# A graph network with a mixture of experts on one core: router spread and biases in packs of four row groups, and z added to x by transfers

## The reference, cut to what matters

```python
x = x + gnn(layernorm(x), ...)                 # the kernel keeps the two terms apart: x and z
t = layernorm(x)
hs = gelu(t @ sw1.T + sb1);  shared = hs @ sw2 + sb2.sum(0)       # 2 shared experts, width 64
probs = softmax(t @ gate_w.T + gate_b)                            # 8 experts
cw = probs where among the two largest, else 0                    # weights of a node
hr = gelu(t @ rw1.T + rb1);  routed = sum_e cw[e] * (hr[e] @ rw2[e] + rb2[e])
out = x + shared + routed
```

## Time and profile before

| | |
|---|---|
| runs, median (lowest to highest) | 1684.27 us (1680.18 to 1685.67) |
| profiled execution, its own time | 1692.14 us |
| its span, from first to last instruction | 1690.4 us |
| TensorE busy in the span, granted clock | 94%, 0.987 |
| VectorE, ScalarE, POOL busy | 54%, 43%, 30% |
| expert stage | about 983 to 1690 |

### The profile page before, as it was taken

The page is one execution under the profiler, slowest core; times in us unless marked ns, Lnnn a source line. Parts: engine busy times, 40 slices in busy tenths (PEclk is TensorE's granted clock), DMA queues, the critical chain, the costliest instruction groups (busy, mean ns, idle before and its releaser), DMA issues. The chain is left out here.

```text
span 1690.4 us, 24020 instructions
## 1 busy us (share of the span) xinstructions
PE 1592.6 (94%) x7903; PEld 1256.2 (74%) x7903; DVE 917.8 (54%) x2179; ACT 724.9 (43%) x1169; POOL 505.5 (30%) x570
## 2 busy tenths in 40 slices
PE   3999999989898999999999868999999999999998
PEld 2677766777785677778887747878888888888887
DVE  4555686967732333347655436664556555655543
ACT  2344435656531222235655324444344534443442
POOL 3572232567732000003665322221112211221100
PEclk9999999999999999999999978999999999999999
DMA  8999999577759999996777750311132113211201
GB/s 259 266 280 280 299 294 271 163 176 125 127 64 290 291 277 282 281 285 192 131 131 143 148 135 34 125 75 75 75 133 93 75 75 125 99 75 75 87 26 44
DMA packets 74133, 273.85 MB, mean 162 GB/s; under 512 B 12726, under 2 KB 12740, under 8 KB 58930
## 3 DMA queue, kind: packets, MB, share of 16 engines
q1 hardware_dynamic: 52530, 223.36, 41.4%
q0 software_dynamic: 21504, 49.26, 16.0%
HBM read 179.82 MB, written 92.76 MB: 161 GB/s over the span
## 5 line engine op out<-in xcount | busy, mean ns | idle before, releaser
L888 POOL TENSOR_TENSOR zr<-zr,xr 128x2048 f32<-128x2048 f32 (+1 forms) x19 | 89.3, 4703 | 414.1 <-DMA xr<-in_x 396.5
L927 ACT ACTIVATE th<-bank 128x512 fp32r<-128x512 f32 x158 | 94.4, 597 | 185.5 <-PE bank L1161 185.3
L1141 PE MATMUL bank<-tth,w1h 128*128 128x512 f32 (+1 forms) x400 | 165.6, 414 | 8.1 <-ACT gel L1064 8.1
L1141 PE MATMUL bank<-ttl,w1h 128*128 128x512 f32 (+1 forms) x400 | 157.8, 395 | 0.0
L1141 PE MATMUL bank<-tth,w1l 128*128 128x512 f32 (+1 forms) x400 | 156.9, 392 | 0.0
L1141 PE MATMUL bank<-w2h,gth 128*128 128x512 f32 x395 | 155.2, 393 | 0.5 <-DVE gtl L1656 0.5
L1141 PE MATMUL bank<-w2h,gtl 128*128 128x512 f32 x395 | 154.7, 392 | 0.0
L1141 PE MATMUL bank<-w2l,gth 128*128 128x512 f32 x395 | 154.3, 391 | 0.0
L1141 PE MATMUL bank<-root2h,th 128*128 128x512 f32 x316 | 132.2, 418 | 8.2 <-DVE yout L1456 4.6
L1141 PE MATMUL bank<-root1h,th 128*128 128x512 f32 x316 | 131.8, 417 | 7.0 <-DVE yout L1456 4.6
L1427 DVE SCALAR_TENSOR_TENSOR tl<-bank,th 128x512 fp32r<-128x512 f32 x79 | 54.5, 690 | 154.1 <-ACT th L927 154.0
(11 more groups left out here) (213 smaller groups left out, 3797.1 us busy)
## 6 DMA issues: line engine op xcount, KB each, us to landing
basis_t<-in_gnn_basis SPq DMA_DIRECT2D x64, 896.0 KB
xin<-in_x SPq DMA_DIRECT2D x39, 512.0 KB, 7.6
xin<-y SPq DMA_DIRECT2D x39, 512.0 KB, 7.1
xr<-in_x SPq DMA_DIRECT2D x19, 1024.0 KB, 6.9
zr<-z SPq DMA_DIRECT2D x19, 1024.0 KB, 4.9
out<-zr SPq DMA_DIRECT2D x19, 1024.0 KB, 3.9
y<-yout SPq DMA_DIRECT2D x37, 512.0 KB, 7.5
z<-yout SPq DMA_DIRECT2D x34, 512.0 KB, 6.8
```

Of the source, the lines that this page charges most:

```text
L888: pool.tensor_tensor(zq, zq, xr[:, q.mod(2), 0:n, :], ALU.add).then_inc(s_zx, 1)
L927: act.activation(th_a[:, s, :], tpb[s][:], f).then_inc(s_hi, 1)
L1141: ins = pe.matmul(out_ap, a(k), b(k), start=first, stop=last)
```

## The change

- **Spread.** `cw3` holds the 30 numbers four times, once in each stretch of 32 columns, so that its transpose has them in four groups of 32 rows. `sel`, the biases `b2` and the mask `lo_row` are copied to rows 32 to 127 by nine transfers of SP. The four spreads stand in one place, behind up product 1, each with 32 rows of its own and a bank of its own (bank 7, both `wb`, `cnt`).
- **Biases.** The four bias matmuls of a group stand together ahead of the first down product, again with 32 rows and a bank each.
- **x and z.** Groups 0 to 2 are summed as before. From group 3 on (`FIRST`) SP loads x straight into `zr`, and POOL adds z to it by an accumulating transfer (`add_z`) in place of `add_x`. The wait for the late rows goes from SP to POOL.
- **Tail.** POOL issues the tail's transfer ahead of 1/sigma of group 1.

The tail's transfer has passed the 1/sigma of group 1, and the second sum, of group 3, has become a transfer. The diff, cut to its core:

```diff
-        cw3 = sb("cw3", [P, QT, 3, NR2])
+        cw3 = sb("cw3", [P, QT, 4, P // 4])
+        spreadb = [bank[7], *wb, cnt]
...
+        def z_added(eng, q):
+            if q.i is None and q.k < FIRST:
+                eng.wait_ge(s_zx, q.k + 1)
+            else:
+                wait(eng, s_zadd[q.mod(4)], q.div(4).times(16, 16 if q.mod(4) == 3 else 0))
...
             zero_late_rows(1)
+            sp.wait_ge(s_sm2, 16 * (2 + FC + 6))
+            for r in range(1, 4):
+                rows = slice(32 * r, 32 * r + 32)
+                for t in (sel[:].bitcast(F32), b2[:], lo_row[:]):
+                    sp.dma_start(t[rows], t[0:32]).then_inc(s_sm2, 16)
...
-            late2_added(sp)
             def group(q):
                 if q.i is not None or q.k > 0:
                     store_group(q + (-1))
-                load_group(q + 3)
+                load_group(x, q + FIRST)
...
             def group(q):
-                if not missing(q + 3):
-                    add_x(q + 3)
+                if not missing(q + FIRST):
+                    add_z(q + FIRST)
...
+            def add_z(q):
                 wait(pool, s_zin[q.mod(4)], q.div(4).times(16, 16))
+                pool.dma_start(zr[:, q.mod(4), 0:tiles_of(q), :], q_rows(z, q),
+                               accum_op=ALU.add).then_inc(s_zadd[q.mod(4)], 16)
...
-            group_rstd(Pos(1))
             pool.wait_ge(s_y, 2 * NT)
             pool.dma_start(z[TAIL + again:N, :], scratch[again:P, :], accum_op=ALU.add).then_inc(s_late2[4], 16)
+            group_rstd(Pos(1))
             pool.wait_ge(s_cw3, 1)
             add_x(Pos(2))
+            late2_added(pool)
             walk_groups(pool, group)
...
-            def spread(q, c):
+            def spread(q):
                 n = tiles_of(q) * P
-                if c == 1:
-                    wait(pe, s_ct, q.times(1, 1))
-                wait(pe, s_gs, q.times(NE // 2, c - 1))
-                pe.matmul(cnt[:, 0:n], sel[:, 2 * c - 2:2 * c, :].rearrange("p e f -> p (e f)"), cwt[:, q.mod(2), 0:n],
-                          start=True, stop=True).then_inc(s_bc, 1)
+                wait(pe, s_ct, q.times(1, 1))
+                wait(pe, s_gs, q.times(NE // 2))
+                wait(pe, s_oe, q.times(QT, 2 - QT))
+                for r in range(4):
+                    rows = slice(32 * r, 32 * r + 32)
+                    ins = pe.matmul(spreadb[r][:, 0:n], sel[rows, 2 * r:2 * r + 2, :].rearrange("p e f -> p (e f)"),
+                                    cwt[rows, q.mod(2), 0:n], start=True, stop=True)
+                ins.then_inc(s_bc, 1)
 
             def logits(q):
...
+                wait(pe, s_gs, q.times(NE // 2, 1 - NE // 2))
...
+            def biases(q):
+                wait(pe, s_oe, q.times(QT))
+                wait(pe, s_gs, q.times(NE // 2, 3))
+                for j in range(tiles_of(q)):
+                    rows = slice(32 * j, 32 * j + 32)
+                    pe.matmul(downb[j][:], cwt[rows, q.mod(2), j * P:(j + 1) * P], b2r[rows, :], start=True, stop=False)
...
             def down(q, j):
-                wait(pe, s_oe, q.times(QT, j - 3))
                 o = downb[j][:]
-
-                pe.matmul(o, cwt[:, q.mod(2), j * P:(j + 1) * P], b2r[:], start=True, stop=False)
...
-                    if c:
-                        spread(q, c)
+                    if c == 1:
+                        spread(q)
...
                 if not missing(nxt):
                     logits(nxt)
+                biases(q)
```

More of the change, by code:

```diff
@@ L341, in gnn_moe_kernel @@
         s_zx = sem("z_plus_x")
+        s_zadd = [sem(f"z_added{i}") for i in range(4)]
         s_qst = sem("group_stats")
@@ L499, in missing, with q_rows @@
             return q.i is None and q.k >= NQ
+        FIRST = 3
+        def q_rows(table, q):
+            if q.i is None and q.k == NQ - 1:
+                return table[N - QLAST * P:N, :].rearrange("(p j) d -> p j d", j=QLAST)
+            groups = table[0:QT * P * (NQ - 1), :].rearrange("(q p j) d -> q p j d", p=P, j=QT)
+            if q.i is None:
+                return groups[q.k]
+            return groups[bass.ds(q.times(1), 1)].rearrange("q p j d -> p (q j) d")
+        def z_added(eng, q):
[3 more added lines that the diff above has]
+                wait(eng, s_zadd[q.mod(4)], q.div(4).times(16, 16 if q.mod(4) == 3 else 0))
         block = ctx.enter_context(nc.Block())
@@ L632, in _, with load_group @@
             load_experts()
[L635 to L647, removed]
+            def load_group(table, q):
+                if missing(q):
                     return
[L649 to L653, removed]
                 wait(sp, s_ost[q.mod(4)], q.div(4).times(16))
-                sp.dma_start(zr[:, q.mod(4), 0:n, :], q_rows(z, q)).then_inc(s_zin[q.mod(4)], 16)
+                sp.dma_start(zr[:, q.mod(4), 0:tiles_of(q), :], q_rows(table, q)).then_inc(s_zin[q.mod(4)], 16)
             def load_x(q):
-                n = q_tiles(q)
                 wait(sp, s_zx, q.times(1, -1))
-                sp.dma_start(xr[:, q.mod(2), 0:n, :], q_rows(x, q)).then_inc(s_xr[q.mod(2)], 16)
+                sp.dma_start(xr[:, q.mod(2), :, :], q_rows(x, q)).then_inc(s_xr[q.mod(2)], 16)
             def store_group(q):
-                n = q_tiles(q)
+                n = tiles_of(q)
                 wait(sp, s_oe, q.times(QT, n))
@@ L677, in _ @@
             scattered(sp, 1)
-            for q in range(2):
-                load_z(Pos(q))
-            load_group(Pos(2))
-            late2_added(sp)
+            for q in range(FIRST):
+                load_group(z, Pos(q))
+            load_x(Pos(2))
             def group(q):
@@ L1617, in router_tiles @@
                     dve.tensor_copy(gwp[:, k, :], zeros[:, 0:P])
-                for i in range(2):
-                    ins = dve.tensor_copy(cwt[:, i, :], zeros[:])
-                link(ins)
+                link(dve.tensor_copy(cw3[:].rearrange("p j r c -> p (j r c)"), zeros[:]))
                 link(dve.tensor_copy(gwp[:, :, 0:NE], gw[:]))
                 dve.tensor_tensor(gwp[:, :, NE:2 * NE], gw[:], gwp[:, :, 0:NE].bitcast(F32), ALU.subtract)
-                dve.memset(cw3[:, :, 0:2, :], 1.0)
-                dve.memset(cw3[:, :, 2, :], 0.0).then_inc(s_qs, 1)
+                for i in range(2):
+                    ins = dve.memset(cw3[:, :, :, i * NR2 + NE:(i + 1) * NR2], 1.0)
+                ins.then_inc(s_qs, 1)
                 dve.wait_ge(s_qs, 1)
@@ L1701, in route_b @@
                 wait(dve, s_cwt, q.times(1))
-                chain(dve.tensor_copy(cw3[:, 0:n, 0, 0:NE], cwh[:, 0:n, :].bitcast(F32)))
-                chain(dve.tensor_copy(cw3[:, 0:n, 1, 0:NE], cwh[:, 0:n, :].bitcast(F32)))
-                chain(dve.tensor_tensor(cw3[:, 0:n, 2, 0:NE], cw[:, 0:n, :], cwh[:, 0:n, :].bitcast(F32), ALU.subtract))
+                full, high = (t.rearrange("p j (a e) -> p j a e", a=1).to_broadcast([P, n, 4, NE])
+                              for t in (cw[:, 0:n, :], cwh[:, 0:n, :].bitcast(F32)))
+                chain(dve.tensor_copy(cw3[:, 0:n, :, 0:NE], high))
+                chain(dve.tensor_copy(cw3[:, 0:n, :, NR2:NR2 + NE], high))
+                chain(dve.tensor_tensor(cw3[:, 0:n, :, 2 * NR2:2 * NR2 + NE], full, high, ALU.subtract))
                 dve.sem_inc(s_cw3, 1)
```

23 lines of the change are left out of this document (12 added, 11 removed).

## The result

The changed kernel took 1658.13 us, the median of four runs (1653.82 to 1661.87), against 1684.44 before (a fourth run beside the three of above); the ratio is 0.9847 (95% interval 0.9825 to 0.9869), 26 us less. The forecast was 1654.7 with a range of 1641 to 1668. In the profiled executions, 1692.14 became 1661.87: 30.3 less, where 29.6 were forecast.

A forecast was written before the change was run, and what follows sets the result against it. The prediction took TensorE's stream to bound steady expert groups, with further losses at the stage's start and in groups 1 to 3: 13.8 + 11.1 + 4.7 = 29.6 us off 1684.3 gives 1654.7, range 1641 to 1668.

The forecast's parts named there:

- The pack's price: Spreads and biases in steady groups: a row pack costs 0.55 us in place of four slots of 0.912, saving 0.36.
- the dense part: TensorE's steady stream of expert groups: 38 packs at 0.36 us and a last one at 0.13 save 13.8 us.
- R1: Rival, packs: perfect overlap, packs save 26 us, total 42 less, so 1642; chance 0.17.
- R2: Rival, packs: their loads go singly, packs save 1 us, total 17 less, so 1667; chance 0.17 with R6.
- R4: Rival, packs: four matmuls don't overlap and each drains, 1.8 us a pack, 18 slower, 1702; chance 0.03.
- R6: Rival, packs: not formed, matmuls run as full ones at 0.228 us each, 1668; chance 0.17 with R2.
- The start: Start of expert stage: earlier tail transfer 8.9 us, four spread banks 1.7, group 0's spreads 0.5; sum 11.1 us.
- The additions: POOL's additions: stalls of 4.7 us in groups 1 to 3 go; in steady groups they hide behind TensorE, nothing.
- The check on new waits: Packs' new waits: the stretch from up 4 to down 0's 13th matmul, needing VectorE's last gtl, stays about equal.
- R3: Rival, groups 1 to 3: stalls return through accumulating transfers' descriptors against VectorE, 1659, or 1665 with half the start's gain; chance 0.10.
- R5: Rival, z addition: needs over 29 us; at 31 it costs 2 us in each of 16 groups, 1687; chance 0.03.
- the copies' "nothing": Nine small SP copies of selection, biases and mask: 3 us of issues, all beside the edges, costing nothing.

The follow-up runs named there:

- full rows: The changed kernel with each spread and bias as a matmul over all 128 rows, without row groups or the nine copies: 1670.03 us, ratio 0.9944 to before.
- pair kernels: The changed kernel with the spread pack cut into two packs of two, behind up products 1 and 2: 1668.19 us, ratio 0.9896 to before.
- second execution of the changed kernel: The changed kernel run once more, unedited, on one chip beside another kernel: 1656.73 us, ratio 0.9848 to before.
- late addition: The kernel before with POOL doing 1/sigma of group q+2 ahead of the addition for group q+3, nothing else: 1682.03 us, ratio 0.9996.
- packs only: The kernel before with only the spread and bias packs; x, z and the tail's transfer as before: 1688.88 us, ratio 1.0046.
- packs and tail: The changed kernel with x and z as before, both loaded and added on POOL: 1679.93 us, ratio 0.9968 to before.

## Why the prediction was right, and where it was not

**The pack's price** was right: 0.55 forecast from the column pack; 0.53 measured as that one was, 0.58 by the intervals of the full rows, and 0.57 for one more of them. The interval forecast, 33.14, is the one measured, so the dense part gave 4 x 0.72 + 10.1 + 0.6 = 13.6 us where 13.8 were forecast. What overlaps, the loads too, is read from four loads in 0.19 us. R1 (perfect packs), R2 (single loads), R4 (no overlap) and R6 (no packs formed) are out by that row and by the full-row and pair kernels. The statement of the Trainium skill in "TensorEngine Tiling (Array Packing)", Tiling Modes, that a change of mode drains the engine fits, though no row shows the drain itself: the pack begins 0.32 behind the matmul ahead of it, not 0.228, and what follows waits until 0.44 after the pack's start, more than a slot. By the 3.07x in the Trainium skill's "TensorE: Matmul & The Clock Gate", Part 3, a pack is an estimated 0.30; among full-row matmuls it took nearly twice that here.

**The start** was right in its order and a little small: 11.1 forecast, 13.0 measured for the first interval. Expected were 999.4 for the table's load (999.08), 1003.6 for the use of exp (1003.30) and tn 0.3 late for the wider copies (cw3's three take 0.24, 0.24 and 0.30 in the chain, where they took 0.19, 0.19 and 0.20: 0.2 more). That the absolute times agree is partly luck: the stage began 1.0 later. Up to the turned weights 10.3 of the 13.0 are gained (8.9 forecast), behind them 2.7 (2.2 forecast). What the sum left out is the clock. It came back during group 0's logits in the changed execution and in the middle of up 0 before, so the stage's first logits to the last matmul of up 0 took 5.9 us, not 7.3. In the second execution of the changed kernel the clock is full from the first logits on, the same stretch takes 4.5 and the interval is 27.13, so 1.4 us either way is scatter of the clock, and no gain of the change is shown in it.

**The additions** were the term that went wrong in kind. As a size, 4.7 us were read from one execution and taken for all; made alone, the transfers are worth 1.2 us (-2.0 to 4.4) and the late addition 0.7. That is of the size of the 3.3 us by which the medians missed, 26.3 against 29.6; with scatter of this size it is not shown to be the same 3.3. The place was a little off too: the 4.7 lie in groups 2 to 4, not 1 to 3, and 1.7 of them are the clock in group 4, which the prediction counted as already full. As a mechanism, the prediction said that in steady groups the additions hide behind TensorE and changing them gives nothing. True of the kernel before, false of the packed one: there they cost what the packs gain, and more (packs only is 7.7 us slower than before, packs and tail 20 slower than the changed kernel). The forecast came out since both parts were made together; so its split, 13.8 for the packs and 4.7 for the additions, is not what either would have given alone, and that the total hid this was luck. The step that failed is "nothing" for the steady groups' additions. The check on new waits, "about equal" for the stretch up to down 0, could not catch it: I watched the last gtl, and the gtl that moved against POOL was that of chunk 2, 0.7 us later against the logits since the spreads between it and them had gone. R3 is out for the changed kernel: its stalls did not come, no gtl is long beside an accumulating transfer; they came with POOL's additions, in kernels that keep them. R5 is out: the addition lands in 8.0 us, not 12, and nobody waits.

Not settled: why the changed kernel's layers 1 and 2 took 1.0 us more in the profiled execution. The eight profiled executions with the nine copies reach the first logits at 989.7 on the mean, the five without at 988.3, within a scatter of 11 us; so the copies' "nothing" is neither shown nor refuted to better than a microsecond or two.

## What to carry to other kernels

Row groups overlap fully here, matmuls and loads, but a pack has a fixed price of 0.53 to some 0.6 us among full-row matmuls (the more, the further behind it one looks); four in a pack win, two don't. A collision between two engines that a slack of half a microsecond hides is part of the price of every edit that moves the stream: look at where the long instruction of the other engine starts relative to each instruction it can block, not only whether anyone waits today. With the packs, exchanging two steps of POOL's program was worth as much here (26 us) as replacing its additions by transfers (20 us); the exchange together with the tail's transfer was not run. And a part that gives nothing alone can be what another part needs, so price it beside the other.

## What the runs showed of the hardware that was not expected

- An order of 0.03 to 0.09 us between two starts decided over some 4.4 us of VectorE and 2.7 us of TensorE: gtl first by 0.03, it took 0.69; POOL's addition first by 0.09, gtl took 5.06.
- In the packs-only kernel the two cases lie clearly apart: in five groups the addition starts 5.9 to 7.0 us ahead of the (delayed) logits, and the gtl of chunk 2 is long; in the eleven others it starts 2.4 to 4.1 ahead, and only the gtl of chunk 3 is. The kernel before has the first case once, in the group that its interval of 36.08 ends with, and in no steady group.
- A 1 MB addition from DRAM onto SBUF landed in 8.0 us (median of sixteen, the longest 8.9; one of 768 KB took 7.0) beside a busy TensorE, and the plain load of 1 MB in 4.9.
- A wait of 2.5 us in a full stream of TensorE was followed by the low clock in one group of the packs-only kernel and not in others: 0.95 over the 34.87 us behind the wait of 2.45, 1.00 over the intervals behind the waits of 2.49, 2.65 and 2.69. Where it came it cost another 1.7 us.
- Two matmuls in a row pack took 0.50 us from first start to last end, four took 0.51.
